# A Mamba scan loop: ScalarE empties two convolution banks one item earlier

## The reference

```
u, z   = split(x @ in_proj_w)                  # 256 + 256 channels
u      = silu(conv3(u) + conv_b)               # depthwise over time, 3 taps
delta, b, c = split(u @ x_proj_w)              # 256, 16 and 16
delta  = softplus(delta @ dt_proj_w + dt_proj_b)
h_t    = exp(delta_t * a) * h_{t-1} + delta_t * b_t * u_t   # 16 states per channel
y_t    = sum over states of h_t * c_t
out    = ((y + u * D) * silu(z)) @ out_proj_w
```

## Time and profile before

| | us |
|---|---|
| median of 3 runs | 1406.0 (1404.15 to 1406.97) |
| the profiled execution | 1406.63 |
| its span | 1404.9 |
| busy over the span: PE, DVE | 1099.2, 1104.9 |
| busy over the span: ACT, POOL | 885.8, 936.7 |

### The profile page before, as it was taken

One profiled execution on the slowest core, in us unless ns is written; L12 is line 12 of the kernel. 1 busy time (PEld: TensorE's weight loads), 2 busy tenths in 40 slices (PEclk: granted clock), 3 DMA queues, 4 the chain that ended last, 5 costly groups with the idle time before them and its releaser, 6 DMA issues. The chain is left out here.

```text
span 1404.9 us, 15371 instructions
## 1 busy us (share of the span) xinstructions
PE 1099.2 (78%) x4128; PEld 508.5 (36%) x4128; DVE 1104.9 (79%) x1448; ACT 885.8 (63%) x1605; POOL 936.7 (67%) x501
## 2 busy tenths in 40 slices
PE   4767877787777877777778876437998989999796
PEld 2322222222222222222222221125655336666695
DVE  6499999999999999999999999885482962222288
ACT  3577577677677577667667665344333876666796
POOL 0199999999999999999999999721010740000176
PEclk9888899989999899989988898856899999999898
DMA  5645835835835835834834846100000001111013
GB/s 158 139 104 120 176 68 120 175 77 110 175 75 112 181 73 108 181 84 97 181 83 98 182 85 157 52 20 1 1 0 14 10 1 34 39 39 34 12 31 91
DMA packets 48490, 122.87 MB, mean 87 GB/s; under 512 B 5824, under 2 KB 20928, under 8 KB 42304
## 3 DMA queue, kind: packets, MB, share of 16 engines
q1 hardware_dynamic: 46864, 121.01, 38.9%
q10 hardware_dynamic: 1584, 1.36, 0.3%
HBM read 83.55 MB, written 5.24 MB: 63 GB/s over the span
## 5 line engine op out<-in xcount | busy, mean ns | idle before, releaser
L555 POOL TENSOR_TENSOR states<-b_dup,dup 128x1024 f32<-128x1024 f32 x256 | 597.0, 2363 | 65.7 <-DMA dup<-dd 64.0
L648 DVE TENSOR_TENSOR_SCAN da<-da,states 128x1024 f32<-128x1024 f32 x160 | 359.5, 2283 | 39.0 <-ACT da L397 33.0
L397 ACT ACTIVATE da<-dup,decay 128x510 f32<-128x510 f32 x512 | 327.2, 672 | 11.1 <-DVE states L648 11.1
L295 PE MATMUL yp<-states,fold 128*64 128x512 f32 x1024 | 275.8, 665 | 15.7 <-DVE states L574 9.8
L534 POOL TENSOR_TENSOR states<-states,X 128x1024 f32<-128x1024 f32 x96 | 226.6, 2360 | 20.8 <-DVE states L648 20.6
L648 DVE TENSOR_TENSOR_SCAN states<-da,states 128x1024 f32<-128x1024 f32 x96 | 218.7, 2278 | 7.0 <-ACT da L397 7.0
L574 DVE TENSOR_TENSOR states<-da,X 128x1024 f32<-128x1024 f32 x160 | 192.5, 1203 | 0.0
L1642 POOL TENSOR_SCALAR put<-row_t,slot_i,slot_w 128x256 f32<-128x256 f32 x32 | 39.1, 1222 | 193.5 <-POOLq L1346 173.5
L393 ACT ACTIVATE da<-zeros 128x4 f32<-128x4 f32 x177 | 30.6, 173 | 197.0 <-DVE states L574 196.3
L295 PEld LDWEIGHTS yp<-states,fold 128*64 128x64 f32 x1024 | 69.3, 152 | 213.0 <-issue 196.5
L1447 DVE TENSOR_TENSOR hx<-glx,upx 128x512 f32<-128x512 f32 x64 | 41.3, 684 | 126.6 <-ACT glx L1412 118.2
(11 more groups left out here) (183 smaller groups left out, 1766.0 us busy)
## 6 DMA issues: line engine op xcount, KB each, us to landing
b_dup<-bc_rows SPq DMA_DIRECT2D x32, 1024.0 KB, 9.5
dup<-dd SPq DMA_DIRECT2D x128, 256.0 KB, 11.7
X<-bc_rows SPq DMA_DIRECT2D x64, 512.0 KB, 11.5
out<-X SPq DMA_DIRECT2D x3, 1024.0 KB, 5.1
wg<-in_wgT SPq DMA_DIRECT2D x16, 128.0 KB, 2.1
wu<-in_wuT SPq DMA_DIRECT2D x16, 128.0 KB, 2.2
wd<-in_wdT SPq DMA_DIRECT2D x16, 128.0 KB, 2.2
bc_rows<-bcf SPq DMA_DIRECT2D x16, 64.0 KB, 1.6
```

The source lines that it names most:

```text
L295: last = nc.tensor.matmul(yp[64 * i:64 * i + 64, :], fold[:], states[:, (2 * step + i) % RING, s, :], start=False, stop=(q == 3 and s == S ...
L397: ins = nc.scalar.activation(factors[:, s, :].rearrange("p (b t) -> p b t", b=2)[:, :, 1:S], src[:, :, 1:S], ACT.Exp, scale=decay[:, col:c ...
L555: nc.gpsimd.tensor_tensor(states[:, i % RING], b_dup[:, par, s0:s0 + SPI, :], dup[:, par, 1, h, g, :].unsqueeze(1).broadcast_to([P, SPI, N ...
L648: nc.vector.tensor_tensor_scan(to.rearrange("p s t -> p (s t)"), factors.rearrange("p s t -> p (s t)"), ring.rearrange("p s t -> p (s t)") ...
```

## The change

On ScalarE the evacuation of CONV1 moves from behind the factors of items 0 and 1 to between them, and the evacuation of CONV0 moves from behind the factors of items 14 and 15 to between them. The variable `no` (the place of the stage in the bank's sequence) is computed earlier in the step. No other engine's program changes.

```diff
@@ scalar engine's body @@
                 for s in range(STEPS):
+                    no = place(n, s - 1)
                     for i in (2 * s, 2 * s + 1):
                         decays(n, par, uses, first, last, i)
+                        if i == 0 and not last:
+                            evacuate(CONV1, n + 1, 1 - par, 8 if first else 8 * n + 7)
                         if i == 6 and not last:
                             log(n + 1)
-                    no = place(n, s - 1)
+                        if i == 14 and not is_at(n, PAIRS - 2, PAIRS - 1):
+                            evacuate(CONV0, n + 2, par, no)
                     if s == 0:
                         if last:
...
                         else:
-                            evacuate(CONV1, n + 1, 1 - par, 8 if first else 8 * n + 7)
                             act.wait_ge(mp_free, 9 if first else 8 * n + 8)
                             nc.scalar.activation(uz[:, par, :, :], uz[:, par, :, :], ACT.Silu).then_inc(silu_done, 1)
                         nc.scalar.preload_act_table_set(LOG_EXP)
...
                     elif s == CONV0 + 1:
-                        if not is_at(n, PAIRS - 2, PAIRS - 1):
-                            evacuate(CONV0, n + 2, par, no)
+                        pass
```

## The result

| | before | after |
|---|---|---|
| median of 5 runs, us | 1404.15 (1402.15 to 1406.97) | 1414.58 (1413.11 to 1420.84) |
| ratio, 95% interval | | 1.0097 (1.0071 to 1.0124) |
| a second set, ratio | | 1.0111 (1.0087 to 1.0135) |

The change made the kernel slower, by 1.0% to 1.1%. Of 1404 us the two ratios are 13.6 and 15.6 us; the sum on record had 16.5. 1414.58 lies in the range of 1411 to 1434. The second set, the changed kernel timed again, had a median of 1417.87.

A forecast was written before the change was run, and what follows sets the result against it. VectorE, with what ScalarE hands to it, was taken to set the pace, GpSimd following. CONV1's move adds 1.18 us in 14 pairs, 16.5 us, CONV0's nothing: 1406.0 becomes 1422.5 us, range 1411 to 1434.

The forecast's parts named there:

- The chain: At each pair's seam, from VectorE's gate through CONV1 and Silu to item 2's scan; VectorE arrives early and waits.
- 1.18 a pair: Item 1's two Exp now stand between CONV1's evacuation and the table load: scan 2 1.18 us later, 14 pairs, 16.5 us.
- The 1.18 doesn't depend on this: How long ScalarE waits for CONV1 doesn't alter the 1.18 us, since it is counted from the end of the matmul.
- CONV0's delay is swallowed: Scan 15 starts 1.61 us later, but VectorE's wait at item 2 shrinks from 2.00 to 1.58; no cost alone.
- The earlier evacuation releases nothing: CONV0's evacuation ends at 484.97 in both orders; CONV1 starts behind the sums with 1.07 us of slack; TensorE gains 0.
- the first pair: CONV1 computed long before there, so the order of the three pieces doesn't change their sum; not among the 14 pairs.
- Rival 1: TensorE's clock stays low behind the longer idle before DELTA: (1.18 + 0.71) x 14 = 26.5 us, 1432.5; chance 0.10.
- Rival 3: GpSimd, busy 97% of the loop, sets the pace, so ScalarE's delay vanishes: no change, 1406 us; chance 0.05.
- Rival 4: CONV0's evacuation frees the accumulator so CONV1 starts sooner: 14 x 0.89 = 12.5 us faster, 1393.5; chance 0.07.
- The total: Whole kernel: 14 x 1.18 = 16.5 us slower, 1422.5 us; forecast's chance 0.75.

The follow-up runs named there:

- Z1 four times: Z1's matmul run four times: on the kernel before, 1382.16 us, ratio 0.9872; on the changed kernel, 1389.50 us, ratio 0.9922.
- CONV0 run early: Kernel before, with TensorE running CONV0 directly behind Z1, ahead of the skip matmul: 1382.99 us, ratio 0.9876; with CONV1's evacuation also between items 0 and 1, 0.9877.

## Why the prediction was right, point by point

- **The chain** (gate, TensorE to CONV1, evacuation, load, Silu, load, item 2's factors). Shown: the one move on it makes the whole effect (1.0101 of 1.0097 to 1.0111), the one off it none (0.9997).
- **1.18 a pair.** Measured from CONV1's evacuation to item 2's scan: 1.19, in every pair. Over the 14 pairs' lengths it is 1.14 and 1.29. 1.3 of the 2.1 us between the two profiles is the first seam's wait at item 15, ahead of the cut; the rest is when CONV1 ended: 10.46 behind the gate in two pairs of each profile, where item 2 waited only 0.72, and up to 13.2 in others, with 1.6 to 1.8 at item 15.
- **Wrong in detail: "The 1.18 doesn't depend on this".** It doesn't where ScalarE would have waited for CONV1 behind item 1's factors. Where CONV1 is done sooner the move costs less: 0.30 a pair with Z1 four times, nothing with CONV0 run early.
- **CONV0's delay is swallowed.** Shown by its move alone. The prediction's 1.61 at item 15 is 0.48 to 1.82 in the two profiles of the changed kernel, and missing in two of the 14 seams of each, where it had a wait in every one.
- **The earlier evacuation releases nothing.** Shown by CONV1's end, 12.36 behind the gate in the mean before, 12.34 and 12.40 after.
- **Wrong in detail: the first pair.** The prediction had its CONV1 long computed. ScalarE waited 0.34 for it already before, at 69.15; the stretch of the earlier trace rows begins at 79.50, although pair 0's item 0 is scanned at 68.18, so that this wait was not in the count of 28. After the change item 1's scan of pair 0 waits 1.32 and item 2's 2.52 (before 0 and 1.90). With CONV1's move alone neither grew (0 and 1.47), as item 0's factors there waited for a DMA. So a fifteenth pair can pay, and the sum lacks it.
- **Rival 1 (a longer idle holds the low clock).** It did slow DELTA: 3.21 in place of 1.98 in this seam. No wait followed at items 3 to 6 of pairs 1 to 14, in either profile, so the price that it named stayed 0. The long waits at item 10 in 7 pairs instead of 5 cost 1.5 us; whether the change brought them, by the phase of the clock, is not shown.
- **Rival 3 (GpSimd sets the pace).** Not in this kernel: its waits went from 18.7 to 37.0 and the loop got longer. It is near only at 51.0 a pair, 1.4 below the kernel before.
- **Rival 4 (the evacuation frees the bank for an earlier CONV1).** It did not happen: CONV1 ended where it had ended before. Where TensorE's work was moved, not ScalarE's, the gain was there.
- **The total.** The measured ratio is 13.6 to 15.6 us, the prediction's 16.5. The number is a little high, the mechanism right. The difference of the profiled loops, with pair 0, is 18.9 and 19.8; that of whole runs is smaller, and the runs of one kernel spread by 5 to 9 us. The longer runs have the lower mean granted clock: 0.885 in the changed kernel's run of 1420.84, 0.888 to 0.890 in its four of 1413.11 to 1415.4. That fits more pairs with an early CONV1 in the short runs, but I can't say which, as timed runs carry no such rows.

## What to carry to other kernels

An engine's wait for a result is a place to put other work into: work ahead of a wait is hidden in it, the same work behind it lies on the chain. Moving a consumer earlier is free only when its producer is already done by then; find out when the producer ends, and if it is late, move the producer. And add a delay to the path only up to the next wait: a delay of 0.5 to 1.5 us in each pair cost nothing, since the wait behind it shrank by as much.

## What the runs showed of the hardware

The granted clock behind a short idle time was worth more than the change under study. Z1's matmuls run four times in place of once cut the idle time ahead of the skip matmul from 3.59 to 1.27 us, the skip and sums that follow took 2.92 instead of 5.40 (granted clock 1.00 instead of 0.80 up to CONV1's end), and the kernel was 1.3% faster with more work on TensorE. A fourth of that stood at another place, item 10. The idle time alone does not tell what follows it: in one trace the softplus matmuls took 6.76 us in one pair and 3.70 in another behind the same 3.25 us of idle. The Trainium skill (TensorE: Matmul & The Clock Gate, "What's actually happening") has activity as what lifts the clock from its resting level; the repeated matmuls agree.
